# A slot stage in four lanes, second routing in two parts, and nine tiles routed early, in a chain of attention, MoE, slot attention and MoE

## Chip, cores, metric

One core of a Trainium2 chip, one launch, fp32 throughout. The metric is the time of one execution in device microseconds; lower is better.

## The reference

x is 16 batch tiles of 128 tokens by 128 features. Each of four layers takes a layer norm of x and is added back to it.

```python
x = x + block(layernorm(x), cond, ctx)       # adaLN self-attention, cross-attention on 77 rows of ctx (16 heads of 64), gated feed-forward
x = x + moe_a(layernorm(x))                  # shared expert + top 2 of 7, each silu(h g') * (h u') d, inner size 352
x = x + slot_attention(cond, ctx, layernorm(x))
x = x + moe_b(layernorm(x))                  # top 1 of 8, relu(h W1 + b1) W2 + b2, inner size 512

def slot_attention(x_cls, x, noise):         # x = ctx: 77 rows; noise: 128 slots for each batch tile
    k, v = ln(x) @ wk + bk, ln(x) @ wv + bv
    slots = q_mu + exp(q_logsig) * noise
    for _ in range(3):
        prev = slots
        q = ln(slots) @ wq + bq
        attn = softmax(k q' * sqrt(D), over slots) + 1e-8
        attn = attn / attn.sum(over rows)
        slots = (attn' v) @ wu + bu + prev
        slots = gelu(ln(slots) @ w1 + b1) @ w2 + b2 + slots
        slots = ln(slots + x_cls)
    return slots
```

## The kernel before

**Engines and order.** Every engine has its own program, and they meet at semaphores. What each does, and in which order, is written out by hand.

**Attention phase (up to about 550 us).** Iteration i works on four batch tiles at once: self-attention of tile i, cross-attention of tile i-1, the feed-forward and the norm for the router of tile i-2, and the projections of tile i+1. Each iteration has twelve steps k; `FILL` says at which step TensorE puts which product into a rotating bank of PSUM, `AT` at which step the other engines take it. `PLAN` works out, from `FILL`, which use of which bank each is. Iterations 16 and 17 drain the streams. VectorE makes maxima, sums and differences, ScalarE exponentials and copies, GpSimd the normalised probabilities (L1954) and the roots for the norms (L1894). The values of the cross-attention go to DRAM (`v_all`, issued by SyncE at L452) and come back tile by tile (L458). In front of them in SyncE's queue stand `pad_a` and `pad_b`, which fill the row tables `rows_a` and `rows_b` in DRAM.

**Routing.** `routing(x, part)` is a generator on VectorE, one small instruction per step: it takes the best experts of each token, ranks the tokens of an expert (two matmuls on TensorE, `rank_sums`) and gives each row a place in `rows_x`. For MoE a it comes in `PARTS`: tiles 0 to 11 inside the attention phase (`early_routing`, around iteration `RANK_AT` = 14), tiles 12 to 15 behind it. GpSimd scatters the rows to their places (`scatter_one`, L1924), two scatters a tile: those of the early tiles one per step from iteration 16 on, the others before the first blocks. For MoE b all tiles are routed in one part.

**Expert blocks.** `rows_a` has a region of 16 blocks for each expert and is 118 blocks of 128 rows long; 38 of them are computed (`step_a`). `rows_b` is dense: 23 blocks, all computed (`step_b`). SyncE reads where a block starts and whose it is from a table in SBUF and loads rows and weights (`load_blocks`). Behind each block GpSimd keeps its metadata (`meta`), casts the destination to an integer (`dest`), waits for the cast, and scatters the result with an indirect DMA (`send_back`, L2016).

**Slot stage (about 675 to 870 us).** The 16 tiles are four groups of four. `LANES` puts two groups into a lane, and each engine does its steps lane by lane, in a loop over the rounds. For a lane a round is: statistics, root (GpSimd), shift `nbias` (L1707), norm on ScalarE (L1168), turn and logits on TensorE, maxima, exponentials with their sums on ScalarE, shares (L1745 reciprocal, L1748 scale and + 1e-8), update on TensorE, new slots, statistics and norm, the MLP with Gelu (L1194), the sum behind it (L1783), statistics, centring with the gain (L1713) and the slots (L1720). One group of each round is normalised by VectorE (`normed_here`). GpSimd takes the roots with `pow`, keeps slots + bias for the next sum (`keep_slots`, `keep_mid`), and adds MoE a's result to x for half of the tiles; VectorE does the other half (L1832). At the end come x + slots, the norm, the gate (logits taken at L1854), the routing of MoE b, 16 scatters, 23 blocks, and the output.

## Time and profile before

| | |
|---|---|
| median of 3 runs | 981.95 us (979.82 to 982.86) |
| the profiled execution's own time | 977.38 us |
| its span in the trace | 975.6 us |
| mean granted clock of TensorE | 0.889 |
| busy: PE / DVE / ACT / POOL | 770.0 / 584.4 / 509.1 / 388.4 us |
| instructions: PE / DVE / ACT / POOL | 5945 / 1939 / 1078 / 563 |

The span is the time between the first and the last record of the profiled execution; busy times are sums over the instructions of an engine within it. The three runs lie 3.04 us apart from lowest to highest. TensorE is PE, VectorE DVE, ScalarE ACT, GpSimd POOL and SyncE SP.

### The profile page before, as it was taken

To read this page: it belongs to the slowest core of one execution; us is meant where nothing else is said; L and a number is where in the kernel's file an instruction comes from. 1 tells how busy PE (TensorE), PEld (TensorE's weight loads), DVE (VectorE), ACT (ScalarE), POOL (GpSimd) and SP (SyncE) were. 2 spreads that over 40 slices of the span, in tenths; PEclk is the share of its full clock that TensorE was granted. 3 is DMA by queue.
4 is the path that set the end of the run, shared out by engine and by line. 5 is a ranking of instruction groups with operands and counts; after the bars stand their busy time and mean duration, and the time that the engine had idled before them with its cause. 6 is when DMAs were issued, how large, how long until landed. Compare 5 with 4: busy or idle time off the path is not lost.

```text
span 975.6 us, 18523 instructions
## 1 busy us (share of the span) xinstructions
PE 770.0 (79%) x5945; PEld 650.1 (67%) x5945; DVE 584.4 (60%) x1939; ACT 509.1 (52%) x1078; POOL 388.4 (40%) x563
## 2 busy tenths in 40 slices
PE   5898899999999999999777699999363645550692
PEld 5677778788888788887665459998242534340692
DVE  2477778777767666568754443333869687763012
ACT  2566677666677666676444223335364545530461
POOL 1234354333333333332337333656624344225453
PEclk9799999999999999999897799999677677765796
DMA  9592011000011001010001136885300000002463
GB/s 264 182 352 94 1 36 36 14 23 28 2 35 36 15 16 34 2 35 28 14 6 37 68 99 174 253 244 167 106 1 1 0 0 0 0 1 76 127 198 106
DMA packets 43155, 70.95 MB, mean 73 GB/s; under 512 B 5339, under 2 KB 28587, under 8 KB 42651
## 3 DMA queue, kind: packets, MB, share of 16 engines
q1 hardware_dynamic: 39579, 62.64, 21.1%
q0 software_dynamic: 3488, 7.20, 2.1%
q8 instruction: 48, 0.79, 0.3%
q14 instruction: 40, 0.33, 0.1%
HBM read 56.53 MB, written 22.67 MB: 81 GB/s over the span
## 4 chain that ended last, share of the span: by engine, by line
PE 46%; DVE 21%; issue 14%; POOL 9%; ACT 5%; DMA 2%; SPq 2%; DVEq 0%; POOLq 0%; ACTq 0%
PE bank L568 5%; PE bank L839 5%; PE bank L630 5%; PE bank L593 3%; DVE sb_smax L1376 3%; PE bank L583 3%; DVE sb_row_sum L1386 3%; PE bank L618 3%; PE bank L574 2%; PE bank L602 2%; PE bank L847 2%; PE bank L659 2%; PE bank L970 2%; DVE sb_st_all L1680 2%; POOL sb_rstd_all L2052 2%
## 5 line engine op out<-in xcount | busy, mean ns | idle before, releaser
L1954 POOL TENSOR_TENSOR sb_expd<-sb_expd,sb_rden 128x512 f32<-128x512 f32 (+1 forms) x128 | 112.6, 880 | 270.3 <-DVE sb_rden L1390 270.1
L1376 DVE TENSOR_REDUCE sb_smax<-bank 128x4 f32<-128x512 f32 (+1 forms) x128 | 74.1, 579 | 63.6 <-PE bank L593 38.8
L618 PE MATMUL bank<-sb_eye,sb_expd 128*128 128x128 f32 (+1 forms) x512 | 78.2, 280 | 6.9 <-POOL sb_expd L1954 6.2
L1080 ACT ACTIVATE sb_expd<-sb_shifted 128x512 f32<-128x512 f32 (+1 forms) x128 | 69.8, 545 | 21.0 <-DVE sb_shifted L1379 19.6
L1386 DVE TENSOR_REDUCE sb_row_sum<-sb_expd 128x4 f32<-128x512 f32 (+1 forms) x128 | 72.9, 570 | 10.9 <-ACT sb_expd L1080 10.9
L1074 ACT ACTIVATE sb_probT<-bank 128x512 f32<-128x512 f32 (+1 forms) x128 | 74.3, 590 | 9.1 <-PE bank L618 8.8
L618 PEld LDWEIGHTS bank<-sb_eye,sb_expd 128*128 128x128 f32 (+1 forms) x512 | 59.9, 146 | 28.3 <-POOL sb_expd L1954 13.9
L1379 DVE TENSOR_TENSOR sb_shifted<-bank,sb_smax 128x512 f32<-128x512 f32 (+1 forms) x128 | 74.9, 585 | 4.4
L893 PE MATMUL bank<-sb_eye,sb_z_all 128*128 128x128 f32 x96 | 24.3, 420 | 66.9 <-ACT sb_z_all L1168 66.9
L568 PE MATMUL bank<-sb_h1T,sb_watt 128*128 128x128 f32 x512 | 72.6, 289 | 4.5 <-DMA sb_watt<-att_w 2.3
L630 PE MATMUL bank<-sb_probT,sb_v 128*64 128x128 f32 (+1 forms) x1024 | 71.2, 282 | 5.5 <-issue 4.0
L568 PEld LDWEIGHTS bank<-sb_h1T,sb_watt 128*128 128x128 f32 x512 | 64.6, 199 | 9.1 <-DVE sb_xb L1365 3.6
L1168 ACT ACTIVATE sb_z_all<-sb_S,sb_nbias,sb_rstd_all 128x128 f32<-128x128 f32 x84 | 33.6, 481 | 62.0 <-DVE sb_nbias L1707 62.0
L630 PEld LDWEIGHTS bank<-sb_probT,sb_v 128*64 128x64 f32 (+1 forms) x1024 | 55.6, 138 | 14.6 <-issue 5.4
L893 PEld LDWEIGHTS bank<-sb_eye,sb_z_all 128*128 128x128 f32 x96 | 17.5, 214 | 71.5 <-ACT sb_z_all L1168 71.2
L2052 POOL TENSOR_TENSOR sb_rstd_all<-sb_rsq_all,sb_halves 128x8 f32<-128x8 f32 x22 | 36.7, 1669 | 59.2 <-DVE sb_rsq_all L1695 59.1
L839 PE MATMUL bank<-sb_blk_xT,sb_up_w 128*128 128x128 f32 x456 | 57.1, 275 | 0.0
L839 PEld LDWEIGHTS bank<-sb_blk_xT,sb_up_w 128*128 128x128 f32 x456 | 54.0, 192 | 0.0
L2016 POOL DMA_INDIRECT back_a<-sb_blk_y,sb_dest x38 | 37.1, 976 | 40.0 <-DVE sb_blk_y L1657 21.7
L1648 DVE TENSOR_TENSOR sb_hid<-bank,sb_hid 128x384 f32<-128x384 f32 x38 | 21.2, 558 | 51.1 <-ACT sb_hid L1129 32.6
L602 PE MATMUL bank<-sb_g,sb_h2T 128*128 128x308 f32 x128 | 48.4, 461 | 0.0
L1659 DVE TENSOR_TENSOR sb_blk_y<-bank,sb_b2b 128x128 f32<-128x128 f32 x23 | 6.7, 291 | 64.0 <-PE bank L978 52.1
(251 smaller groups left out, 1886.9 us busy)
## 6 DMA issues: line engine op xcount, KB each, us to landing
sb_up_w<-gate_up SPq DMA_DIRECT2D x38, 384.0 KB
rows_a<-pad_a SPq DMA_DIRECT2D x1, 7670.0 KB, 26.8
sb_up_w<-w1b SPq DMA_DIRECT2D x23, 256.0 KB
sb_v<-v_all SPq DMA_DIRECT2D x16, 308.0 KB
v_all<-sb_v_rows SPq DMA_DIRECT2D x9, 512.0 KB, 2.6
sb_blk_x<-rows_a SPq DMA_DIRECT2D x38, 65.0 KB
sb_watt<-att_w SPq DMA_DIRECT2D x4, 512.0 KB, 6.3
sb_picked<-back_a SPq DMA_DIRECT2D x4, 512.0 KB, 5.4
```

The source lines that it names most:

```text
L568: mm = pe.matmul(t[:, c * n:(c + 1) * n], w[:, (4 * half + c) * P:(4 * half + c + 1) * P], src, start=True, stop=True)
L602: pe.matmul(score[u % 2][:, :, 0:C], h2T[:, :], g2[:, QH * j:QH * (j + 1), first:first + C], start=True, stop=True).then_inc(score_done, 1)
L618: mm = pe.transpose(trans[u % 2][0:n, h, :], expd[:, (units_before(i) + u) % EXP_RING, h, 0:n], eye[:, :])
L630: mm = pe.matmul(pvo[DH * r:DH * r + DH, h, :], v[:, 8 * (j // 2) + 2 * h + r, :], probT[0:n, (u - 1 + r) % 2, h, :], start=True, stop=True)
L839: mm = pe.matmul(bank[1 + 2 * j + v][:, c * P:(c + 1) * P], up_w[:, (u + 1) % NSLOT, (j * CA + c) * P:(j * CA + c + 1) * P], blk_xT[:, v, ...
L1074: act.activation(probT[0:n, u % 2, :, :], trans[u % 2][0:n, :, :], ACT.Copy).then_inc(probT_ready, 1)
L1080: act.activation(expd[:, (units_before(i) + u) % EXP_RING, :, 0:n], shifted[:, u % 2, :, 0:n], ACT.Exp, scale=DH ** -0.5).then_inc(exp_don ...
L1376: dve.tensor_reduce(smax[:, u % 2, :], s_in, X, ALU.max).then_inc(max_done, 1)
L1379: dve.tensor_tensor(shifted[:, u % 2, :, 0:n], s_in, smax[:, u % 2, :].unsqueeze(2).broadcast_to([P, QH, n]), ALU.subtract).then_inc(sub_d ...
L1386: dve.tensor_reduce(row_sum[:, u % 2, :], expd[:, (units_before(i) + u) % EXP_RING, :, 0:n], X, ALU.add).then_inc(row_sum_done, 1)
L1954: pool.tensor_tensor(e, e, rden[:, u % 2, :].unsqueeze(2).broadcast_to([P, QH, n]), ALU.mult).then_inc(norm_done, 1)
L2052: pool.tensor_tensor(rstd_all[:, c], rsq_all[:, 0, c], halves[:, c], ALU.pow).then_inc(sl_root, 1)
```

## The change

**Sizes and parts.** MoE a: nine tiles are routed early, seven late. The steps of early routing come one per step k, begin in iteration 10 and end in 13 (`RANK_AT` = 12), and its 18 scatters go out in iterations 14 and 15 from step 4 on (`SCATTER_FROM`). MoE b: two parts, tiles 0 to 11 and 12 to 15; `rows_b` gets a region of 16 blocks for each expert, like `rows_a`, and is 135 blocks long; its table of starts (`start["b"]`) is made as for a, and `w1b` is padded by an expert of zeros. `PLAN` moves the rank matmuls to step 1 of iteration 12 and VectorE's taking of them to step 2; `AT["exp"]` goes from 9 to 5.

**Slot stage.** Four lanes of one group each. `SLOT_STEPS` gives every step a phase; `slot_steps` sorts the steps of all rounds and groups by it, and each engine does its own steps in that order, with the loops written out. Every step waits for its own group: one semaphore for each kind of step. All groups are normalised by ScalarE. The sum behind the MLP is made by TensorE, which multiplies `s_rest` by the identity into the bank of the second layer; statistics and centring read the bank. Shares and the variance + eps are `scalar_tensor_tensor` with a tensor (`least`, `eps`) where a constant was. The sums of x are all VectorE's.

**Routing.** A step of the generator now waits for its result when it is taken up again (`pause`), not before it yields. **Send back.** The destination is cast for each block when its metadata is kept, into a column of its own, and the scatter waits only for the block's result.

```diff
-NREG = EA * REGION + NR - 2 * TOK // P
-
-PARTS = {"a": ((0, 12), (12, B)), "b": ((0, B),)}
+NREG = {"a": EA * REGION + NR - 2 * TOK // P, "b": EB * REGION + NB - TOK // P}
+
+PARTS = {"a": ((0, 9), (9, B)), "b": ((0, 12), (12, B))}
...
-RANK_AT = [last + 2 for _, last in PARTS["a"][:-1]]
+SCATTER_FROM = 4
+RANK_AT = [last + 3 for _, last in PARTS["a"][:-1]]
+SLOT_STEPS = {
+    (-1,): {"add": 7.75},
+    range(0, SLOT_ITERS + 1): {"measure_q": 4.51, "root_q": -0.32, "shift_q": 4.59, "norm_q": 0.96, "turn_q": -6.50,
+        "scale_q": 1.07},
+    range(SLOT_ITERS): {"logits": -6.11, "max": 5.25, "exp": 1.53, "shares": 5.58, "update": -5.64, "updated": 5.96,
+        "keep_mid": 1.75, "measure_m": 6.24, "root_m": 1.42, "shift_m": 6.51, "norm_m": 2.61, "turn_m": -4.62,
+        "scale_m": 3.04, "layer1": -4.37, "gelu": 3.16, "layer2": -3.76},
+    range(-1, SLOT_ITERS): {"measure_o": 7.90, "root_o": 2.80, "centre": 8.12, "slots": 8.38},
+    range(-1, SLOT_ITERS - 1): {"keep_slots": 3.66},
+    (SLOT_ITERS,): {"gate": -5.63, "gated": 8.50, "choose": 9.01, "rank": 69.64, "choice_exp": 70.64, "place": 9.99,
+        "send": 10.95},
+}
+ROUTING_AT = {"choose": (2, 3), "rank": (2, 3), "place": (2, 3), "choice_exp": (3,)}
+
+def slot_steps(*names):
+    found = [(4 * (it + 1) + g + phases[name], name, it, g) for its, phases in SLOT_STEPS.items() for name in names
+             if name in phases for it in its for g in ROUTING_AT.get(name, range(4))]
+    return [step[1:] for step in sorted(found)]
...
-        rows_b = nc.dram_tensor("rows_b", (NB * P, ROW), F32, kind="Internal").ap()
+        rows_b = nc.dram_tensor("rows_b", (NREG["b"] * P, ROW), F32, kind="Internal").ap()
...
+                if step == "layer2":
+                    pe.wait_ge(mid_rest, nth(it, g))
+                    pe.wait_ge(hid_ready, nth(it, g))
+                    for n, b in enumerate(tiles(g)):
+                        pe.matmul(quads(bank[2 * g])[:, n, :], eye[:, :], s_rest[:, b, :], start=True, stop=False)
+                        mm = pe.matmul(quads(bank[2 * g])[:, n, :], hid[:, b, :], w2s, start=False, stop=True)
                     mm.then_inc(mlp_done, 1)
...
-                for part, rank_at in enumerate(RANK_AT):
-                    if (i, k) == (rank_at - 1, N_STEPS - 1) or i == rank_at and k < 6:
-                        steps(early[part], 2)
-                    if i == rank_at and k == AT["rank"]:
-                        steps(early[part], 1)
-                    if i == rank_at + 1:
-                        steps(early[part], 2)
+                for part, rank_at in enumerate(RANK_AT):
+                    if (i, k) == (rank_at - 2, N_STEPS - 1) or i == rank_at - 1:
+                        steps(early[part], 1)
+                    if i == rank_at and k >= AT["rank"] or i == rank_at + 1:
+                        steps(early[part], 1)
...
+                dve.scalar_tensor_tensor(rsq_all[:, 0, c], mv_all[:, c, 1], 1.0, eps[:, c], ALU.mult, ALU.add).then_inc(var_ready[k], 1)
...
+                if step == "shares":
+                    dve.wait_ge(att_exp, nth(it, g))
+                    link(dve.reciprocal(rsum[0:C, c], esum[0:C, c]))
+                    for b in tiles(g):
+                        ins = dve.scalar_tensor_tensor(att[:, b, :], att[:, b, :], rsum[0:C, b:b + 1], least[0:C, :], ALU.mult, ALU.add)
+                    ins.then_inc(att_ready, 1)
...
-                dve.tensor_tensor(group(S, g), quads(bank[2 * g])[:, :, :], group(s_rest, g), ALU.add).then_inc(sum_ready, 1)
...
+                if step == "centre":
+                    scale = es_b[:, :] if it < 0 else R["lnp_g"]
+                    src = x_sb if it < 0 else SUMS
+                    for b in tiles(g):
+                        ins = dve.scalar_tensor_tensor(S[:, b, :], row(src, b), mv_all[:, b, 0:1], scale, ALU.subtract, ALU.mult)
+                    link(ins)
...
-                    if (i, k) == (rank_at + 2, 0):
+                    if (i, k) == (rank_at + 2, SCATTER_FROM):
...
-                    n = N_STEPS * (i - rank_at - 2) + k
-                    if n in range(2 * (last - first)):
+                    n = (N_STEPS - SCATTER_FROM) * (i - rank_at - 2) + k - SCATTER_FROM
+                    if k >= SCATTER_FROM and n in range(2 * (last - first)):
                         scatter_one("a", n % 2, first + n // 2)
...
-                        pool.tensor_copy(meta[:, bass.ds(m, 1), :].rearrange("p a n -> p (a n)"),
-                                         blk_x[:, r, D:ROW]).then_inc(meta_kept[x], 1)
+                        pool.tensor_copy(meta[:, m, :], blk_x[:, r, D:ROW])
+                        stand()
+                        pool.tensor_copy(dest[x][:, m:m + 1], blk_x[:, r, D:D + 1]).then_inc(meta_kept[x], 1)
...
-                        from_one(pool, returned[x][r], 16 * (q - (u == 0)))
-                        stand()
-                        pool.tensor_copy(dest[:, r:r + 1], meta[:, bass.ds(m, 1), 0:1].rearrange("p a n -> p (a n)")).then_inc(
-                            dest_ready[x], 1)
-                        pool.wait_ge(dest_ready[x], m + 1)
                         pool.wait_ge(y_ready[x], m + 1)
...
+                if step == "send":
+                    pool.wait_ge(routed["b"], 1 if g < 3 else 2)
+                    pool.wait_ge(z_normed["q"], nth(it, g))
+                    for b in tiles(g):
+                        scatter_one("b", 0, b)
```

## Rows read from the trace of the kernel before

**Rows 1.** windows, attention: us, then PE PEld DVE ACT POOL busy, PEclk, DMA, GB/s:

```profile
442.00:469.00 27.00, 24.70 (x205) 20.28 (x204) 22.14 (x57) 17.80 (x34) 9.10 (x12) 1.00 0.08 25
469.00:503.50 34.50, 26.17 (x217) 22.39 (x217) 25.82 (x72) 17.12 (x30) 9.98 (x16) 0.85 0.04 11
```

**Rows 2.** timeline of VectorE, attention phase: start, duration, engine, line, operation, wait before it:

```profile
451.92 1.15 DVE L1419 SCALAR_TENSOR_TENSOR sb_rt<-sb_rt,sb_rows 128x84 f32<-128x84 f32 x1
...
524.66 0.34 DVE L1359 TENSOR_SCALAR sb_zC<-sb_x,sb_mv,sb_rstd 128x128 f32<-128x128 f32 x1 [2.71 <-POOL sb_rstd L1894]
...
548.27 0.18 DVE L1415 TENSOR_REDUCE sb_top<-sb_logits 128x4 f32<-128x28 f32 x1 [2.38 <-POOL sb_z_all L1978]
```

**Rows 3.** windows of core 0, one slot round and the scatters behind it:

```profile
758.40:811.50 53.10, 29.92 (x136) 23.32 (x135) 41.71 (x199) 28.07 (x74) 20.04 (x15) 0.69 0.00 0
...
886.40:909.70 23.30, 0.00 (x0) 0.02 (x1) 0.81 (x3) 0.00 (x0) 15.41 (x16) 0.50 0.30 97
```

**Rows 4.** waits of VectorE, 705 to 865 us: total us, count, longest:

```profile
DVE sb_rsum L1745 <- ACT sb_att_or_sent L1183: 10.3, 6, 3.3
```

**Rows 5.** timeline of GpSimd, two scatters of the second expert blocks:

```profile
944.51 0.97 POOL L2016 DMA_INDIRECT back_b<-sb_blk_y,sb_dest  x1 [0.82 <-POOL sb_dest L2011]
...
963.14 0.97 POOL L2016 DMA_INDIRECT back_b<-sb_blk_y,sb_dest  x1 [0.82 <-POOL sb_dest L2011]
```

**Rows 6.** timeline of TensorE, last second-layer matmuls of the second MoE:

```profile
956.55 1.15 PE L978 MATMUL bank<-sb_w2b,sb_hid 128*128 x8 [0.54 <-DVE sb_blk_y L1659]
```

**Rows 7.** timeline of GpSimd, scatters of the first MoE and the first metadata:

```profile
516.46 1.01 POOL L1924 DMA_INDIRECT rows_a<-sb_att_or_sent,sb_slot  x1 [0.16 <-issue]
...
567.01 1.05 POOL L1924 DMA_INDIRECT rows_a<-sb_sent,sb_slot  x1 [18.40 <-DVEq L1506]
...
584.67 0.83 POOL L2004 COPY sb_meta<-sb_blk_x 128x2 f32<-128x2 f32 x4 [7.76 <-DMA sb_blk_x<-rows_a]
```

**Rows 8.** DMA issues: KB each, us from issue to landing:

```profile
rows_a<-pad_a SPq DMA_DIRECT2D x1, 7670.0 KB, 26.8
...
rows_b<-pad_b SPq DMA_DIRECT2D x1, 1495.0 KB, 31.0
```

**Rows 9.** timeline of SyncE: the store of values and the load behind it:

```profile
65.11 0.33 SPq L452 DMA_DIRECT2D v_all<-sb_v_rows  x1
...
80.96 0.78 SPq L458 DMA_DIRECT2D sb_v<-v_all  x2
```

**Rows 10.** timeline of TensorE: first values of tile 0; first block of experts:

```profile
106.33 1.09 PE L630 MATMUL bank<-sb_probT,sb_v 77*64 77x128 f32 x16 [0.53 <-issue]
...
588.37 0.33 PE L819 MATMUL bank<-sb_eye,sb_blk_x 128*128 128x128 f32 x1 [0.78 <-DVE sb_x L1624]
```

**Rows 11.** groups by line, VectorE, 758.4:811.5: busy us, mean ns | idle before:

```profile
L1720 DVE SCALAR_TENSOR_TENSOR sb_S<-sb_S,sb_rstd_all,sb_rows 128x128 f32<-128x128 f32 x16 | 6.4, 475 | 0.5 <-DVE sb_S L1713 0.5
...
L1713 DVE SCALAR_TENSOR_TENSOR sb_S<-sb_S,sb_mv_all,sb_rows 128x128 f32<-128x128 f32 x16 | 4.4, 345 | 0.0
...
L1748 DVE TENSOR_SCALAR sb_att_or_sent<-sb_att_or_sent,sb_rsum 77x128 f32<-77x128 f32 x16 | 3.5, 277 | 0.1
...
L1783 DVE TENSOR_TENSOR sb_S<-bank,sb_s_rest 128x512 f32<-128x512 f32 x4 | 2.7, 689 | 0.2 <-PE bank L929 0.2
```

**Rows 12.** timeline of VectorE, start and end of the slot stage:

```profile
679.13 0.69 DVE L1832 TENSOR_TENSOR sb_x<-sb_x,sb_picked 128x512 f32<-128x512 f32 x1 [7.49 <-DMA sb_picked<-back_a]
...
869.79 0.17 DVE L1707 SCALAR_TENSOR_TENSOR sb_nbias<-sb_mv_all,sb_rstd_all 128x8 f32<-128x8 f32 x1 [1.87 <-POOL sb_rstd_all L2052]
...
877.12 0.29 DVE L1854 TENSOR_TENSOR sb_logits<-bank,sb_rows 128x128 f32<-128x128 f32 x1 [6.13 <-PE bank L953]
```

**Rows 13.** groups by line and form, GpSimd: the roots of four columns:

```profile
L1901 POOL TENSOR_TENSOR sb_rstd_all<-sb_rsq_all,sb_halves 128x4 f32<-128x4 f32 x6 | 6.1, 1021 | 6.2 <-DVE sb_rsq_all L1257 6.2
```

**Rows 14.** timeline of ScalarE, a table load and the Gelu behind it:

```profile
781.28 1.28 ACT L1194 ACT_TABLE_LOAD   x1
782.57 1.27 ACT L1194 ACTIVATE sb_hid<-bank,sb_cols 128x512 f32<-128x512 f32 x2
```

More of the change, by code:

```diff
@@ L722, in rank_sums @@
                 w = N_EXP[x] * (last - first)
[L723 to L725 removed]
+                src = hot[:, N_EXP[x] * first:N_EXP[x] * first + w]
+                pe.matmul(t[:, 0:w], tri[:, :], src, start=True, stop=True)
+                pe.matmul(t[:, w:2 * w], ones[:, :], src, start=True, stop=True).then_inc(
+                    proj_full if x == "a" and part in range(len(RANK_AT)) else rank_done[x], 1)
             def iteration(i, S):
@@ L956, in _ @@
+                if step == "gate":
+                    pe.wait_ge(zT_ready["q"], nth(it, g))
+                    for n, b in enumerate(tiles(g)):
+                        mm = pe.matmul(bank[2 * g + 1][:, n * EB:(n + 1) * EB], zsT[:, b, :], wgate[:, :], start=True, stop=True)
+                    mm.then_inc(lgb_done, 1)
+                if step == "rank":
+                    rank_sums("b", g - 2, bank[2 * (g - 2)])
+            pe.wait_ge(ranks_kept["b"], len(PARTS["b"]))
             pe.wait_ge(ld_moe_b, 32)
@@ L1156, in _, with normed @@
                 from_slot_bank(vu[:, 4 * g:4 * g + 4, 0:D], lambda t: quads(t)[0:C, :, :])
-            def modulated_group(g, done, count, ready, scale, bias):
-                act.wait_ge(done, count)
-                act.activation(group_of(zsT, g), bank[2 * g][:, :], ACT.Identity, scale=scale, bias=bias).then_inc(ready, 1)
-            def normed(lane, stat, count, ready, src=S, dst=zs, groups=2):
-                act.wait_ge(stat, count)
-                for b in tiles(lane)[:4 * groups]:
+            def normed(it, g, k, src, dst):
+                act.wait_ge(shift_ready[k], nth(it, g))
+                for b in tiles(g):
@@ L1753, in updates @@
[L1753 to L1762 removed]
+            links = [0]
```

643 lines of the change are left out of this document (244 added, 399 removed).

## The prediction

> **What bounds the kernel now.** I read the busy time by windows first, then the timelines of single engines where a window is slow, then the groups of instructions and the waits of the slot stage, last the DMA issues. No engine bounds the whole kernel. The attention phase runs on TensorE, one batch tile per iteration of about 26 us, except where VectorE falls behind: iteration 15 takes 34.5 us with 72 VectorE instructions, against 27.0 us for the one before it [rows 1]. The extra instructions are the early routing of twelve tiles, two per step; several of them take over 1 us where a neighbour of the same size takes 0.3, since both of their inputs are in SBUF and GpSimd is reading too [rows 2]. In the two drain iterations 16 and 17 GpSimd has 24 scatters in its queue, and two things wait behind them: zC for 2.71 us, and the end of the phase for 2.38 us [rows 2].
>
> The slot stage is bound by VectorE plus its waits. One round of 53.1 us has 41.7 us of VectorE, 28 of ScalarE, 20 of GpSimd, and TensorE at a mean clock of 0.69 between its two levels [rows 3]. The waits come from two lanes of eight tiles that leave VectorE nothing to do while a lane's exponentials run [rows 4]. Then comes a serial tail: last norm, gate, routing, 16 scatters with TensorE at a standstill for 23.3 us [rows 3]. In the expert blocks of the second MoE GpSimd is last: its scatters are 2.07 us apart (9 steps between the two rows), and the last one starts 5.4 us after TensorE has finished [rows 5, 6].
>
> **Attention phase.** (a) With nine tiles, routing takes its steps one at a time in iterations 11 to 13, and iteration 15 has none: 34.5 falls to the 27.0 of its neighbour, which carried 12 routing instructions and shows that this many are hidden: -7.5 (bounds -9.5, 0). (b) Iterations 11 to 13 get some 12 each on a VectorE that has 27 - 22 = 5 us left: +0.5 each, +1.5 (0, +4). (c) 18 scatters now start in iteration 14 at step 4, one per step, eight in 14 and eight in 15. A scatter takes 1.01 us and starts 0.16 us behind GpSimd work [rows 7]; what hides it is GpSimd's idle time, about 18 of 27 us; behind it queue the normalisation of the probabilities and the roots of the norms. +1 per iteration, +2 (0, +8). (d) Iterations 16 and 17 lose 22 of 24 scatters: the two waits above end, down to the usual root latency: -1.8 and -2.2, together -4 (-5, -2). (e) rows_b is laid out in regions, so its pad grows from 1495 KB (23 blocks) to 8775 KB (135 blocks). The first pad moves at 7670 / 26.8 = 286 KB/us, so both, 9165 KB, hold the queue for 32 us [rows 8]; the store of values issued at 65.11 us behind them lands only at 80.96, when SP issues the load that waited for it [rows 9]. 7280 KB more are 25 us more: that store lands near 106, its load near 109, and TensorE wants these values at 106.3 us [rows 10]. Nothing else is ready in its queue then: +3 (0, +6). Sum: -7.5 + 1.5 + 2 - 4 + 3 = -5.
>
> **Start of the first blocks.** The late part of routing has seven tiles, 14 scatters for 8. They start at 567.01 and the eighth has ended at 576.9 (584.67 less 7.76 of idle), 1.28 us for each; six more end 7.7 us later, at 584.6 [rows 7]. From there to GpSimd's first metadata it is 7.8 us today, so the blocks would be there at 592.4, and TensorE comes at 588.37 [rows 7, 10]: +4 at most. But part of the 7.8 us is four weight loads (1536 KB, 5 us at the rate above) that by then are done: +2 (0, +4). Inside the blocks TensorE is the bound and nothing changes; at the end the destination is cast earlier, -0.5.
>
> **Slot stage.** VectorE is busy 41.7 us in a round [rows 3]. Off it go the sums after the MLP, 2.7 (TensorE adds s_rest by the identity) and the normalisation of one group, 4 x 0.27 = 1.1 (ScalarE's now) [rows 11]. On it come the tensor form of shares, 4.4 for 3.5 by the row of the nearest instruction of that form [rows 11]; some 14 small instructions of about 0.1, since blocks of four columns replace blocks of eight, 1.5; the waits for its own results in each group, about 1.1, 4.4 in all; and 0.9 for shares that meet GpSimd, half of what the slots instruction pays for that (6.4 against 4.4) [rows 11]. Statistics and centring read PSUM instead of SBUF; the trace has no statistics from PSUM, and I take them as equal (0, +1 a round). Sum 45.6 us a round, 11.4 a group. At the start each group has, at the same rates, two residual sums 1.8, statistics 1.5, centring 1.3, slots 1.3, statistics 1.5: 7.4 us; at the end one sum and a shift: 1. Together 4 x (7.4 + 3 x 11.4 + 1) = 171 us of VectorE. From its first sum at 679.1 to the last shift at 869.9 [rows 12] it is 190.7 us today. What is left as wait in the new order: about 3 us while the first group fills, 5 in the last round, where only one group's chain runs. In the middle the longest gap is from the query shift to the maxima (four norms, turn, scale, four matmuls). For two groups the like chain (norm, turn, copy, gate) took 7.3 us [rows 12]; for one I take 5.5, and between the two steps stand measure_o, updated, centre and measure_m, 5.8 us. So it just closes. 171 + 8 = 179, -11.7 us (-18, +4).
>
> What could break this: a root on GpSimd takes 1.02 us for four columns [rows 13], hidden by the 1.3 us of shares. ScalarE alternates Gelu and Exp in every group, eight table loads a round against two: that makes its round 28.1 + 6 x 1.28 + 1.7 (the fourth group's normalisation) = 37.5 us, 9.4 a group, under 11.4 [rows 3, 14]. The row shows the next activation 0.01 us after a load [rows 14]. The Trainium skill, "ScalarE: Activation LUTs", section What ACT_TABLE_LOAD costs, gives 1.28 us for the load and some 1.38 us of drain with it; this trace has the first number and not the second.
>
> **Tail.** Today the first scatter comes 16.5 us after the last shift and the sixteenth 19 us later. Part 0 (12 tiles) is placed only behind "gated" of group 3: 5.7 for gate, 0.3, ranks on TensorE 0.9, 13 placing instructions 3.3, GpSimd 0.8: first scatter at +11. Part 1 is ready by +15, while part 0's twelve still run. So all 16 scatters stay exposed and only their start moves: -5.6 (-9, -2). The larger table is made beside them.
>
> **Second blocks.** The wait for its own cast goes, and the wait for `returned`. The cast costs 0.82 us of idle time before each scatter, against 0.16 behind work without such a wait [rows 5, 7]. Cycle 0.97 + 0.3 + 0.2 = 1.5, below TensorE's. TensorE ends at 957.7 [rows 6]; with 0.3 for the result, 0.8 and 0.97 the last scatter ends at 959.8, not 964.1: -4.3, and TensorE's own waits of 0.5 go: -4.8 (-6, 0 if the 0.82 stays).
>
> **Sum.** -5 + 2 - 0.5 - 11.7 - 5.6 - 4.8 = -25.6 us. It is made on the profiled execution (977.4 us, span 975.6), which lies 4.6 below the median of the runs; I carry the difference to the median: 981.95 - 25.6 = **956 us**.
>
> **Rivals.**
> 1. The waits are halved only. Today 53.1 - 41.7 = 11.4 us of a round are not VectorE work [rows 3]. If TensorE sits at its lower level and an in-order queue hands the delay on, about 13 more us remain over three rounds: 969. For it: clock 0.69, two to three times more handovers; against it: shorter gaps for TensorE. Chance 0.20.
> 2. No change: all 11.4 us a round stay and VectorE has 45.6 of its own, 57 a round: +34 - 8 = +26, 982. Chance 0.05.
> 3. Slower: VectorE and GpSimd block each other. The slots instruction, with two SBUF inputs, costs 0.40 beside GpSimd's keep_slots, the like centring 0.27 [rows 11]. Shares and eps get two SBUF inputs as well, five such places in a group. If each waits for one whole GpSimd instruction (1.0 to 1.3 us, less what is in the sum), that is 3.6 us per group, x 12 = 43: 999. It decides from 2.1 us per group. The Trainium skill, "SBUF — State Buffer", section Who interferes with whom, has that rule (an exclusive lock for the whole instruction); the rows agree in kind. Chance 0.04.
> 4. ScalarE becomes the bound: with 1.4 us of idle behind each load it needs 9.4 + 2 x 1.4 = 12.2 us a group, 0.9 over VectorE, x 12: 967. The page on ScalarE above would have it so. Chance 0.05.
> 5. Better: the pads and the scatters in 14 and 15 cost nothing (-5), the clock rises and the middle has no wait (-7): 944. Chance 0.11.
>
> **How the numbers follow.** The sum as worked out has 0.55 and a range of its own of 948 to 964. Eight times in ten: 943 to 973, which leaves out rivals 2 and 3 and the ends of 1 and 5. 0.3%, about 3 us, is what a measurement can tell: faster 0.91, within it 0.05 (rival 2), slower 0.04 (rival 3).
>
> **What would show it.** Iteration 15 at 27 us; the store of values landing near 106 and TensorE waiting before that pv matmul; the first block transpose 2 us later against the end of the phase; one max per group every 11.4 to 12 us; in the wait list of VectorE few waits for ScalarE; shares at about 0.27 each; first b scatter 11 us behind the last shift; GpSimd's gap before a back_b scatter gone, and scatters at TensorE's pace. It is wrong if groups follow each other at over 13 us, if slots and shares show long durations beside GpSimd, or if iterations 14 and 15 grow.

## The result, and the profile after

The changed kernel takes 970.08 us (median of 4 runs, 969.70 to 974.45); the kernel before takes 982.40 in the same comparison. The ratio is 0.9879 (95% interval 0.9854 to 0.9903): 12 us faster, where 26 were forecast. The sign is right and the time lies inside the range, but about half of the gain is missing. The profiled execution took 969.92 us, with a span of 968.0.

The spans differ by 7.6 us. The kernel before had been profiled in one of its shorter executions (977.4 against a median of 982.4), so stages are compared by the two traces, and the whole by the medians. Each column of the table is one execution, and the same stage of one kernel differs between executions; where that matters, the spread is given.

The table cuts the span at instructions that both traces have, and gives what each stretch became. The last two columns are of runs told of below: the changed kernel again in another set of runs (r1), and, in that set, the changed kernel with one step of GpSimd moved (r2).

| stretch, us | before | predicted | changed | r1 | r2 |
|---|---|---|---|---|---|
| start to first instruction of late routing | 548.3 | -5.0 | -7.5 | -6.9 | -8.7 |
| to last scatter of the first MoE's blocks | 124.8 | +1.5 | +10.2 | +0.3 | +1.7 |
| to the first sum of x | 6.0 | 0 | +0.3 | +0.4 | +0.3 |
| slot stage, to the last shift | 190.7 | -11.7 | -0.8 | -0.2 | -11.8 |
| to the first scatter of the second MoE | 16.6 | -5.6 | -6.2 | -6.2 | -6.2 |
| to the last scatter of its blocks | 76.7 | -4.8 | -4.1 | -3.4 | -3.3 |
| to the end | 12.5 | 0 | +0.5 | +0.4 | +0.5 |
| span | 975.6 | -25.6 | -7.6 | -15.6 | -27.6 |

Two stretches hold the whole miss: the first MoE's blocks start late, and the slot stage gained nothing.

**Slot stage.** One round of the changed kernel, between two maxima of one group, by windows (columns as in rows 1):

```profile
746.66:798.37 51.71, 34.99 (x169) 27.86 (x167) 44.54 (x205) 37.78 (x85) 22.44 (x21) 0.74 0.00 1
```

Against 53.10 us [rows 3] that is 1.4 less, with VectorE busier (44.54 us for 41.71). The groups of instructions by line of the same window, VectorE (busy us, mean ns):

```profile
L1705 DVE SCALAR_TENSOR_TENSOR sb_att_or_sent<-sb_att_or_sent,sb_rsum,sb_least 77x128 f32<-77x128 f32 x16 | 5.6, 407 | 0.1
...
L1736 DVE SCALAR_TENSOR_TENSOR sb_S<-sb_S,sb_rstd_all,sb_rows 128x128 f32<-128x128 f32 x16 | 4.6, 347 | 0.0
...
L1674 DVE SCALAR_TENSOR_TENSOR sb_nbias<-sb_mv_all,sb_rstd_all 128x4 f32<-128x4 f32 x8 | 4.6, 571 | 0.1
```

The eight shifts of four columns (L1674) take 571 ns on average, where one of eight columns takes 0.17 us [rows 12]. The mean mixes two kinds: three of the eight take 1.25 or 1.26 us, the other five 0.16. The timelines of one group, VectorE, GpSimd, ScalarE and TensorE in turn:

```profile
764.34 0.16 DVE L1674 SCALAR_TENSOR_TENSOR sb_nbias<-sb_mv_all,sb_rstd_all 128x4 f32<-128x4 f32 x1
...
764.62 1.14 DVE L1705 SCALAR_TENSOR_TENSOR sb_att_or_sent<-sb_att_or_sent,sb_rsum,sb_least 77x128 f32<-77x128 f32 x4
765.67 1.25 DVE L1674 SCALAR_TENSOR_TENSOR sb_nbias<-sb_mv_all,sb_rstd_all 128x4 f32<-128x4 f32 x1
...
773.23 0.69 DVE L1698 TENSOR_REDUCE sb_lgmax<-bank 77x4 f32<-77x512 f32 x1 [0.67 <-PE bank L926]
```

```profile
764.45 1.02 POOL L1936 TENSOR_TENSOR sb_rstd_all<-sb_rsq_all,sb_halves 128x4 f32<-128x4 f32 x1 [0.47 <-DVE sb_rsq_all L1668]
765.43 1.47 POOL L1951 TENSOR_TENSOR sb_s_rest<-sb_S,sb_cb 128x512 f32<-128x512 f32 x1
```

```profile
766.96 1.65 ACT L1162 ACTIVATE sb_z_all<-sb_S,sb_nbias,sb_rstd_all 128x128 f32<-128x128 f32 x4 [0.79 <-DVE sb_nbias L1674]
```

```profile
771.28 1.92 PE L926 MATMUL bank<-sb_zsT,sb_kq 128*77 128x128 f32 x8
```

GpSimd's keep_mid (L1951) begins at 765.43 and ends at 766.90. VectorE's query shift, both inputs in SBUF, begins at 765.67 and ends at 766.92, with it. Behind it wait the norm of the queries, the turn, the logits and the maxima. So it is in eleven of twelve groups (1.25 us ten times, 1.11 once); in the twelfth keep_mid comes a little earlier against them, and the shares are held instead, 2.15 us for the four. VectorE and GpSimd:

```profile
750.91 2.15 DVE L1705 SCALAR_TENSOR_TENSOR sb_att_or_sent<-sb_att_or_sent,sb_rsum,sb_least 77x128 f32<-77x128 f32 x4
```

```profile
751.66 1.26 POOL L1951 TENSOR_TENSOR sb_s_rest<-sb_S,sb_cb 128x512 f32<-128x512 f32 x1
```

**First blocks.** VectorE's and ScalarE's timelines at the end of the shared expert, and TensorE's behind it:

```profile
581.10 0.69 DVE L1604 TENSOR_TENSOR sb_x<-sb_x,bank 128x512 f32<-128x512 f32 x1 [9.66 <-remote]
```

```profile
581.15 1.08 ACT L1112 ACTIVATE sb_hid<-bank 128x512 f32<-128x512 f32 x2 [10.51 <-remote]
```

```profile
572.52 3.60 PE L824 MATMUL bank<-sb_zsT,sb_moe_w 128*128 128x512 f32 x8
583.12 5.49 PE L812 MATMUL bank<-sb_moe_w,sb_s_rest 128*128 128x128 f32 x24 [7.01 <-DVE sb_s_rest L1611]
589.39 0.47 PE L843 MATMUL bank<-sb_eye,sb_blk_x 128*128 128x128 f32 x1 [0.78 <-DVE sb_x L1604]
```

Both engines wait for TensorE's matmuls, which by their records are over at 572.7 and 576.1. The semaphore counts that they wait for come at 581.07 to 581.19, three within 0.12 us ("remote": the profile ties the release to no instruction). Meanwhile GpSimd issues its fourteen scatters, from 560.80 to 577.63, and SyncE, which waits until all of them have landed, starts to load rows at 580.10:

```profile
580.10 10.27 SPq L511 DMA_DIRECT2D sb_blk_x<-rows_a  x5
```

TensorE has nothing to do, its granted clock falls, and the next 24 matmuls take 5.5 us. The windows show the clock, the third last number, at 0.50, its lower level of 1.2 GHz:

```profile
576.00:584.00 8.00, 0.99 (x5) 0.88 (x5) 1.97 (x3) 1.08 (x2) 3.23 (x11) 0.69 0.24 66
584.00:590.00 6.00, 5.09 (x23) 4.50 (x22) 0.72 (x2) 0.10 (x1) 0.00 (x1) 0.50 0.00 0
```

The kernel before has one such wait, of 2.3 us, with eight scatters.

**Attention.** Iterations 14 and 15 of the changed kernel by windows:

```profile
439.85:469.67 29.82, 29.25 (x253) 24.43 (x253) 19.56 (x53) 20.59 (x38) 15.01 (x20) 1.00 0.11 34
469.67:500.41 30.74, 22.88 (x213) 19.40 (x213) 19.72 (x54) 16.73 (x30) 17.98 (x24) 1.00 0.09 29
```

**Tail and second blocks.** VectorE's last shift, GpSimd's first scatter of routing b and its last of the blocks:

```profile
871.98 0.16 DVE L1674 SCALAR_TENSOR_TENSOR sb_nbias<-sb_mv_all,sb_rstd_all 128x4 f32<-128x4 f32 x1 [1.24 <-POOL sb_rstd_all L1936]
```

```profile
882.39 1.05 POOL L1814 DMA_INDIRECT rows_b<-sb_sent,sb_slot  x1 [10.56 <-DVEq L1489]
...
955.03 0.95 POOL L1902 DMA_INDIRECT back_b<-sb_blk_y,sb_dest_b  x1 [0.74 <-issue]
```

### The profile page after: what moved, and what is told of

Same layout as the page of the kernel before. It is cut to its first block, busy times and chain, and to the rows that moved or that the text cites. A ratio compares the mean times of both kernels' runs of the same rounds, so it can differ in the third digit from the quotient of the medians.

```text
span 968.0 us, 18773 instructions
## 1 busy us (share of the span) xinstructions
PE 795.7 (82%) x6045; PEld 672.2 (69%) x6045; DVE 592.9 (61%) x1989; ACT 536.7 (55%) x1109; POOL 392.2 (41%) x583
## 4 chain that ended last, share of the span: by engine, by line
PE 48%; DVE 23%; issue 10%; DMA 7%; ACT 5%; POOL 4%; SPq 3%; another core or an unknown queue 1%; DVEq 0%; POOLq 0%; ACTq 0%
PE bank L591 5%; PE bank L653 4%; DMA v_all<-sb_v_rows 4%; PE bank L863 4%; PE bank L616 4%; PE bank L606 3%; PE bank L597 3%; DVE sb_smax L1352 2%; PE bank L641 2%; DVE sb_st_all L1661 2%; PE bank L625 2%; PE bank L969 2%; PE bank L682 2%; PE bank L977 2%; DVE sb_row_sum L1362 2%
## 5 line engine op out<-in xcount | busy, mean ns | idle before, releaser
L1936 POOL TENSOR_TENSOR sb_rstd_all<-sb_rsq_all,sb_halves 128x4 f32<-128x4 f32 x44 | 44.7, 1016 | 92.9 <-DVE sb_rsq_all L1668 92.9
L1362 DVE TENSOR_REDUCE sb_row_sum<-sb_expd 128x4 f32<-128x512 f32 (+1 forms) x128 | 72.9, 570 | 11.3 <-ACT sb_expd L1079 11.2
L931 PE MATMUL bank<-sb_vu,sb_att_or_sent 77*128 77x129 f32 x96 | 21.7, 395 | 48.9 <-DVE sb_att_or_sent L1705 48.9
L863 PE MATMUL bank<-sb_blk_xT,sb_up_w 128*128 128x128 f32 x456 | 59.7, 283 | 0.0
L1162 ACT ACTIVATE sb_z_all<-sb_S,sb_nbias,sb_rstd_all 128x128 f32<-128x128 f32 x96 | 39.5, 482 | 31.7 <-DVE sb_nbias L1674 31.7
L863 PEld LDWEIGHTS bank<-sb_blk_xT,sb_up_w 128*128 128x128 f32 x456 | 56.5, 199 | 0.0
L1902 POOL DMA_INDIRECT back_a<-sb_blk_y,sb_dest_a x38 | 37.0, 973 | 45.1 <-issue 23.7
L931 PEld LDWEIGHTS bank<-sb_vu,sb_att_or_sent 77*128 77x128 f32 x96 | 18.4, 285 | 51.5 <-DVE sb_att_or_sent L1705 51.5
L616 PE MATMUL bank<-sb_k1T,sb_q1T 64*128 64x128 f32 x512 | 38.4, 289 | 5.6 <-DVE sb_shifted L1355 5.0
```

Source lines behind the costliest of these rows:

```text
L616: mm = pe.matmul(score[(u + r) % 2][:, h, :], q1T[p, 4 * (j // 2) + h, :], k1T[p, 4 * (j // 2) + h, :], start=True, stop=True)
L863: mm = pe.matmul(bank[1 + 2 * j + v][:, c * P:(c + 1) * P], up_w[:, (u + 1) % NSLOT, (j * CA + c) * P:(j * CA + c + 1) * P], blk_xT[:, v, ...
L1362: dve.tensor_reduce(row_sum[:, u % 2, :], expd[:, (units_before(i) + u) % EXP_RING, :, 0:n], X, ALU.add).then_inc(row_sum_done, 1)
```

## Experiments

Medians and ratios are those of a set of runs made on one chip, against the kernel before in the same set; each of the four sets was on another chip. Experiments 1 to 4 are one set, 5 to 7 a second, the first three of 8 a third, and its last four a fourth.

**1. The changed kernel again, without an edit.**

> The changed kernel once more, beside which the others of this set are read. Question: is the wait at the end of the shared expert a fixed cost? In its first trace the counts of TensorE that ScalarE and VectorE wait for come at 581.1 us, 8.4 us behind the matmuls by their records, while the four weight loads of the blocks and 14 scatters are under way, and TensorE's granted clock falls to 0.5 behind it. Theory C (collision of that moment's transfers): the wait comes again, 6 to 10 us, since everything is issued at the same moments; 970 us. Rival (a chance stall of one execution): it is gone or of quite another size, and the trace's last block ends some 9 us earlier.

970.33 us, ratio 0.9879 (0.9845 to 0.9913). The wait came again, 9.54 us on VectorE, and the first block was turned at 592.3. So it is no chance of one execution.

**2. keep_mid in front of root_m.** GpSimd takes it while VectorE reads PSUM.

```diff
-        "keep_mid": 1.75, "measure_m": 6.24, "root_m": 1.42,
+        "keep_mid": 1.41, "measure_m": 6.24, "root_m": 1.42,
```

> GpSimd's keep_mid (1.27 us, two inputs in SBUF) moves from behind root_q to in front of root_m, where VectorE reads PSUM. Theory H (holding): in the changed kernel the query shift of a group takes 1.25 us instead of 0.16, ends with keep_mid each time, and the norm of the queries stands behind it. Then the shift falls to 0.16, the chain to the maxima begins 1.1 us earlier, and groups follow each other every 11.7 to 12.0 us instead of 12.8: 9 to 12 us in all, 958 to 961. Rival Q (TensorE's order and clock set the pace): the shift is short, but VectorE waits as much longer for the logits: within 2 us of the changed kernel.

958.99 us, ratio 0.9780 (0.9745 to 0.9816), 11.3 us under the changed kernel of that set. Its query shifts, by groups of instructions on VectorE, and one round by windows:

```profile
L1674 DVE SCALAR_TENSOR_TENSOR sb_nbias<-sb_mv_all,sb_rstd_all 128x4 f32<-128x4 f32 x8 | 1.3, 157 | 0.0
```

```profile
769.50:814.62 45.12, 30.31 (x168) 23.37 (x166) 40.19 (x205) 36.94 (x84) 21.40 (x20) 0.85 0.01 1
```

And keep_mid beside the centring, GpSimd and then VectorE, of its repetition (8 below):

```profile
769.80 1.27 POOL L1951 TENSOR_TENSOR sb_s_rest<-sb_S,sb_cb 128x512 f32<-128x512 f32 x1 [0.30 <-DVE sb_S L1714]
```

```profile
769.64 1.12 DVE L1730 SCALAR_TENSOR_TENSOR sb_S<-bank,sb_mv_all,sb_rows 128x128 f32<-128x128 f32 x4
```

The centring, with one input in PSUM, keeps its 1.12 us beside it. One phase number was worth about as much as the whole change (11.3 us beside 12). The holding theory stands; the rival, that TensorE's order sets the pace, falls.

**3. Twelve tiles early, with the schedule of before.**

```diff
-PARTS = {"a": ((0, 9), (9, B)), ...
-SCATTER_FROM = 4
-RANK_AT = [last + 3 ...
+PARTS = {"a": ((0, 12), (12, B)), ...
+SCATTER_FROM = 0
+RANK_AT = [last + 2 ...
```

with the positions of rank and exp in FILL and AT, and the two steps at a time of early routing, as before.

> Twelve tiles routed early, two steps at a time, scatters in iterations 16 and 17, as in the kernel before; all else as changed. By the traces the attention phase gets its 7.5 us back, and 8 scatters instead of 14 stand before the blocks. Theory C (the stall at the end of the shared expert comes from having more scatters and the weight loads at the same moment): the stall falls back to the 2.1 us of before, so that the blocks begin about as early as in the changed kernel and the sum is +0 to +2 us against it. Rival (the stall is of the code, not of the transfers): it stays at 8 us, +7 us against the changed kernel.

971.48 us, ratio 0.9881 (0.9840 to 0.9922): 1.2 more than the changed kernel of its set. The first late routing comes at 550.1 instead of 544.1, and the longest late count is 0.9 us. Where the counts are late, nine tiles give back at the start of the blocks what they won in the attention phase.

**4. Weights of the first blocks behind the scatters.** SyncE issues the four weight loads last.

```diff
-                for m in range(NSLOT):
-                    load_weights(x, m, places[m][1])
                 sp.wait_ge(scattered[x], 16 * scatters)
                 for m in range(NSLOT):
                     load(x, src, m, places[m][0])
+                for m in range(NSLOT):
+                    load_weights(x, m, places[m][1])
```

(for the first MoE alone).

> In front of the first blocks of the first MoE, SyncE waits for the scatters and loads the rows first, and issues the four weight loads (1536 KB) behind them. Theory C: with the weight loads away from the end of the shared expert the stall of 8.4 us is gone and TensorE's clock stays up (another 5 us), but weights land some 6 us after the last scatter, at 586: the blocks begin near 586 instead of 589.4 at full clock, -5 to -8 us in all. Rival (scatters alone or the fetch of code make the stall): it stays, and the blocks begin later by the load's 5 us, +3 to +5.

971.26 us, ratio 0.9895 (0.9863 to 0.9927). VectorE waits 9.46 us as before, and the block comes at 590.7. The weight loads are not the cause: theory C falls.

**5. Shares and eps with constants.**

```diff
-  dve.scalar_tensor_tensor(att[:, b, :], att[:, b, :], rsum[0:C, b:b + 1], least[0:C, :], ALU.mult, ALU.add)
+  dve.tensor_scalar(att[:, b, :], att[:, b, :], rsum[0:C, b:b + 1], 1e-8, ALU.mult, ALU.add)
```

and the variance + eps likewise.

> The changed kernel with shares and variance + eps written with constants again (tensor_scalar) instead of the tensors least and eps. By the rows shares go from 0.35 to 0.28 us each, 0.28 us a group, 3.4 us of VectorE in all. If VectorE's work sets the pace of the groups it is 3 us faster than the changed kernel (967); if the chain from the query shift to the maxima does (it ends in a wait of 0.67 us for TensorE), nothing moves by more than 1 us. Rival: the constant forms hold GpSimd's roots and the kernel is slower by 3 us or more, which would be the reason for the tensor forms.

970.41 us, ratio 0.9881 (0.9852 to 0.9909): no difference in the median. Its shifts and shares on VectorE:

```profile
L1674 DVE SCALAR_TENSOR_TENSOR sb_nbias<-sb_mv_all,sb_rstd_all 128x4 f32<-128x4 f32 x8 | 4.9, 612 | 0.7 <-POOL sb_rstd_all L1936 0.6
...
L1705 DVE TENSOR_SCALAR sb_att_or_sent<-sb_att_or_sent,sb_rsum 77x128 f32<-77x128 f32 x16 | 3.5, 278 | 0.1
```

Shares take 3.5 us a round where undisturbed tensor forms take 4.5 (the kernel of 2), and all twelve shifts are held, but for 1.03 to 1.10 us instead of 1.25: keep_mid, which in the changed kernel begins 0.3 us before the shares are done and takes 1.47 us, here takes 1.27. Groups follow every 12.6 instead of 12.8 us, and the slot stage of this trace takes 186.3 us, against 189.5 to 191.2 in the seven traces that have the tensor forms and keep_mid in its old place: about the 3.4 us expected. The median does not show them. Five executions lie 5.2 us apart, and the set has no run of the unedited changed kernel, so whether the constant forms gain 3 us in all stays open; the rival, that they cost 3 us, falls.

**6. Scatters in two batches, and scatters held back.** In the first GpSimd waits behind the seventh late scatter until seven have landed; in the second it waits for the end of the shared expert ahead of all fourteen.

```diff
+                    if (b, k) == (first + 3, 0):
+                        pool.wait_ge(scattered["a"], 16 * (2 * b + 1))
```

```diff
+            pool.wait_ge(sh_added, G)
             for b in range(first, last):
```

> The changed kernel, with GpSimd waiting once, behind the seventh of the fourteen late scatters, until all have landed (some 3 us). Theory S (the scatters in flight hold TensorE's counts once they are many): the stall of 8.4 us shrinks to the size seen with eight scatters, 2 us or less, TensorE's clock stays up, and the blocks begin when the scatters have landed, near 583 instead of 589: -5 to -9 us. Rival (the stall belongs to this place of the program whatever the scatters do): it stays, and the whole is 0 to 3 us slower.

> The changed kernel, with all fourteen late scatters held back until the shared expert is done. If scatters cause the stall, no count of TensorE is late in this stretch (none above 1 us), the shared expert ends near 577, and the scatters run alone behind it for 18 us: blocks begin near 598, +7 to +9 us against the changed kernel. If they don't cause it, the stall stays, the shared expert ends at 588 and the blocks begin at 609: +18 to +20.

Two batches: 969.94 us, ratio 0.9864 (0.9834 to 0.9894), none of the 5 to 9 us expected in the median. The long wait is gone from its place, and one of 5.4 us stands at the last down product. It ends when the second batch has landed, at which SyncE loads the rows (VectorE, then SyncE):

```profile
588.74 0.69 DVE L1604 TENSOR_TENSOR sb_x<-sb_x,bank 128x512 f32<-128x512 f32 x1 [5.39 <-remote]
```

```profile
588.74 3.03 SPq L511 DMA_DIRECT2D sb_blk_x<-rows_a  x5
```

The first block is turned at 590.8. Counted from the first instruction of late routing that is 44.0 us, against 48.6 and 48.2 in the two traces of the unedited kernel, and the stretch to the last scatter of the blocks takes 129.2 us against 135.0 and 134.5: the 5 us are there in this trace, but its attention phase took 546.9 us against 540.8 and 544.1. What the batches are worth is therefore not settled by the median.

Held back: 986.78 us, ratio 1.0047 (1.0026 to 1.0068). VectorE's timeline, and TensorE's at the first block:

```profile
573.86 0.69 DVE L1604 TENSOR_TENSOR sb_x<-sb_x,bank 128x512 f32<-128x512 f32 x1 [1.29 <-PE bank L812]
```

```profile
603.97 0.45 PE L843 MATMUL bank<-sb_eye,sb_blk_x 128*128 128x128 f32 x1 [22.36 <-DMA sb_blk_x<-rows_a]
```

No count is late without scatters in flight, at the price of scatters that nothing hides. The 16 us above the changed kernel (of the other sets) are more than the 7 to 9 expected: the shared expert is done only at 582.3, not near 577, so that the scatters run from 583.15 and the first block comes at 604 instead of 598; TensorE stands still for 22 us before it.

Could this run simply have had no late counts, whatever the scatters did, as the runs of 8 below? One sign says no. In the second MoE scatters are in flight too when SyncE reads the table of starts, and its first weight load comes 4.5 to 4.7 us behind the table in every trace of the changed kernel and its variants from the result and experiments 1 to 6, and 3.0 to 3.2 us in all those of 8. In this run it is 4.68 (VectorE, then SyncE):

```profile
906.45 0.17 DVE L1509 TENSOR_TENSOR sb_start_b<-sb_bex,sb_rows 1x23 int32<-1x23 f32 x1
```

```profile
911.13 3.29 SPq L519 DMA_DIRECT2D sb_up_w<-w1b  x4
```

So the scatters are needed for the late counts. That they are not sufficient is what 8 shows.

**7. The edit of send_back alone, in the kernel before** (the diff is that of the change).

> The kernel before with the edit of send_back alone: a column of destinations for each block, cast with the metadata, no wait for the cast or for the returned rows. As in the prediction: scatters of the second blocks at TensorE's pace, the last one 4 to 5 us earlier, the first MoE's blocks unchanged but 0.5 at their end: 4.8 us faster than before (977.5). Rival (the wait is only renamed, since the indirect DMA waits for the block's result anyway): within 1 us of before.

977.90 us, ratio 0.9952 (0.9932 to 0.9973), 3.8 us faster. Most scatters start 0.58 to 0.72 us behind the metadata instead of 0.82 behind their own cast, and they follow each other every 1.9 us. From the first scatter of the second MoE to the last of its blocks it is 72.4 us instead of 76.7. The term holds.

**8. Ten tiles; logits first; pad in parts** (each with keep_mid moved as in 2).

```diff
-PARTS = {"a": ((0, 9), (9, B)), ...
+PARTS = {"a": ((0, 10), (10, B)), ...
```

```diff
-    range(SLOT_ITERS): {"logits": -6.11, ...
+    range(SLOT_ITERS): {"logits": -6.38, ...
```

```diff
+                if 2 <= i < 7:
+                    part = slice((i - 2) * NREG["b"] * ROW // 5, (i - 1) * NREG["b"] * ROW // 5)
+                    sp.dma_start(*(v.rearrange("(p n) d -> p (n d)", p=P)[:, part] for v in (rows_b, A["pad_b"]))).then_inc(zeroed, 16)
...
```

> keep_mid as in e1_keep_mid_early, and ten tiles routed early instead of nine: routing moves one iteration back, its 20 scatters go out in iterations 15, 16 and 17, and 12 instead of 14 stand before the blocks. Theory S (TensorE's counts are late while back-to-back scatters are in flight, from the seventh or eighth on until all have landed): the scatters end 2.5 us earlier, the stall is 2.5 us or more shorter, and the attention phase is up to 2 us longer: -1 to -4 us against e1_keep_mid_early (ratio to before 0.976, 0.972 to 0.977). Rival: the drain iterations lose as much by the scatters in them: ratio 0.978 or above.

> keep_mid as in e1_keep_mid_early, and TensorE makes the logits of a group in front of the first MLP layer instead of behind it. In e1_keep_mid_early VectorE still waits for the logits, 1.0 us in some groups, none in others. Theory Q (the chain from the query shift to the maxima still sets part of the pace): those waits end, -3 to -5 us against e1_keep_mid_early (ratio to before 0.973 to 0.975). Rival (VectorE's own work is the bound now, and ScalarE's Gelu, later by the logits' 1 us, moves the wait to the second layer's statistics): within 1.5 us, 0.977 to 0.980.

> keep_mid as in e1_keep_mid_early, and the 8775 KB of pad_b issued in five parts behind the value transfers of iterations 2 to 6 instead of in one behind pad_a. In the traces with the whole pad the stretch from the first use of the values to the next iteration takes 0 to 4 us more than before (30.5 to 34.5 us), 1.6 in the mean. Theory E (the pad delays the store of values past the moment TensorE wants them): the stretch is 30.5 us again, values of later iterations still come in time, -1 to -2 us in the median against e1_keep_mid_early (ratio to before 0.976 to 0.977). Rival (the parts delay the later values instead): 0 to +5 us.

Ten tiles 954.13, ratio 0.9743 (0.9700 to 0.9785); logits first 950.12, ratio 0.9713 (0.9676 to 0.9750); pad in parts 949.55, ratio 0.9694 (0.9664 to 0.9723). By their ratios the last came 7 us better than expected and logits first 2. The traces show that no count is late in any of the three, though logits first has the same instructions up to the end of the first MoE as kernels that had the wait, pad in parts differs there only in the transfers of the pad, and both issue the same scatters at the same moments (logits first from 560.18 to 577.00). So theory S falls as stated: scatters are not enough. Ten tiles came inside the range expected, but not for the reason given, since there was no late count to shorten. The changed kernel and that of 2 were run once more beside two combinations.

> The changed kernel for the third time. Theory P (the stall goes with the chip or the placement of a call, not with the program): if e11 and e12 of this call show no stall, this one shows none, its blocks begin near 583 and it takes 961 to 964 us against a before of about 979; if they show it, this one does, and takes 970. Rival (program): it shows the 8.4 us and 970 us whatever e11 and e12 show.

> e1_keep_mid_early for the second time, for comparison inside one call. Whatever the stall does, it is 10 to 12 us faster than the changed kernel of this call (theory H). Under theory P its blocks begin when those of r1_changed_third do.

> keep_mid in front of root_m, logits in front of the first MLP layer, and pad_b in five parts; nine tiles. If the parts add up: 0 to -3 us for the logits and -1 to -2 us for the pad against r2_keep_mid_again. Rival: both are within what a call differs from another, and it is within 1 us of r2_keep_mid_again.

> As e11_all_nine, with ten tiles routed early. In e8_ten the drain iterations were some 5 us longer than with nine tiles and two scatters fewer stood before the blocks. If this call has the stall, ten tiles are 1 to 4 us faster than nine; if it has none, 2 to 4 us slower.

The unedited changed kernel took 962.51 us here, ratio 0.9823 (0.9799 to 0.9848), as theory P had it, and its trace has no late count. VectorE's and TensorE's rows at the place of the wait, and the windows:

```profile
573.10 0.69 DVE L1604 TENSOR_TENSOR sb_x<-sb_x,bank 128x512 f32<-128x512 f32 x1 [1.29 <-PE bank L812]
```

```profile
582.55 0.30 PE L843 MATMUL bank<-sb_eye,sb_blk_x 128*128 128x128 f32 x1 [1.71 <-DMA sb_blk_x<-rows_a]
```

```profile
584.00:590.00 6.00, 5.87 (x52) 5.65 (x51) 1.88 (x5) 2.17 (x6) 1.60 (x5) 1.00 0.56 160
```

keep_mid moved: 950.07, ratio 0.9693 (0.9671 to 0.9715), again 12.4 us under the changed kernel of its set. All parts with nine tiles: 950.58, ratio 0.9704 (0.9679 to 0.9730); with ten: 954.14, ratio 0.9715 (0.9679 to 0.9751). Logits first and pad parts together add nothing that can be told, and ten tiles are no better where the counts are in time. The version to keep is the changed kernel with keep_mid moved.

## Why the prediction was off

**Slot stage, forecast -11.7, came -0.8.** The step that failed is the term for VectorE instructions that meet GpSimd, "0.9 for shares that meet GpSimd": I looked for the cost of two SBUF inputs only in large instructions, priced what a held instruction loses itself, and put the small ones at nothing. The one that was held is the smallest there is, the query shift, 1.09 us in ten of the groups (0.95 in another), and it stands at the head of the chain to the maxima. Eleven groups of it make 12 us, the whole gain of the stage. With keep_mid moved the same stage takes 179.2 and 178.8 us for the 179 forecast (kernel of 2 and r2), but that it agrees so well is in part luck. A round was to take 45.6 us each time; between the second and third maxima of a group it takes 45.1 to 46.8, between the first and second 46.8 to 51.7. VectorE is busy for 151.6 us of the stage in both, where the 171 worked out, less the 13 in them for waits for its own results, make 158: the work was put too high by about what the waits were put too low. The mechanism was my rival 3, whose size of 3.6 us a group was three times too large and whose chance of 0.04 was too small, and which named shares and eps and not the shift; below its turning point of 2.1 it does not reverse the sign, and that middle case I had left out. The Trainium skill, "SBUF — State Buffer", section Who interferes with whom, has this rule, that a VectorE instruction with two SBUF inputs contends with a GpSimd instruction that reads SBUF, and that one with at most one SBUF input, outside the two-port modes, does not. The shift (held) and the centring from PSUM (1.12 us beside keep_mid) agree with the two halves. GpSimd's root does not fit the first: it has two SBUF inputs and takes 1.02 us, yet the shares beside it, with two SBUF inputs, take 1.14 us for four (764.62 above), as the slots instruction does with GpSimd idle. Here the measurement decides:

```profile
761.49 1.14 DVE L1736 SCALAR_TENSOR_TENSOR sb_S<-sb_S,sb_rstd_all,sb_rows 128x128 f32<-128x128 f32 x4
```

**Start of the first blocks, forecast +2, came +8.5, and with the low clock behind it +10.2.** The scatters themselves were priced rightly: the first rows are there at 582, and in the runs without late counts the stretch costs +0.3 (r1) and +1.7 (r2). What I had no term for is that TensorE's counts come late while they are in flight. The sum has it at nothing; it measured 8.4 us of lateness, and the first block came 8.5 us later where 2 were forecast. The row was there in the trace of before (ScalarE, 2.3 us, "remote"), and I read past it:

```profile
578.34 0.60 ACT L1113 ACTIVATE sb_hid<-bank 128x512 f32<-128x512 f32 x1 [2.26 <-remote]
```

It is a matter of the set of runs as well as of the program: the changed kernel took 970.1 and 970.3 in two sets with it and 962.5 in one without. That it needs scatters in flight is shown (6); why it is there in some sets and not in others is open, since sets differ in chip and time at once. The two misses add up to more than the whole: with neither of them r2 takes 950.07 us, 6 below the forecast of 956.

**Attention, forecast -5, came -7.5.** The -7.5 is one execution: in the ten traces with nine tiles and the whole pad the phase is 1.4 to 8.7 us shorter than in the trace of before, 6.2 in the mean, so the sum of -5 was about right. Its parts were read less well. (a) The window of 27.0 us that I took for an iteration was a part of iteration 14. By the starts of the same norm in both traces an undisturbed iteration takes 29.3 to 29.6 us, and 14 and 15 took 32.2 and 34.5; they now take 29.8 and 30.7: -6.1 for the -7.5. Iteration 15 goes with TensorE's granted clock, which I had left out: the row of before has 0.85 [rows 1], the changed kernel 1.00. Of the ten traces just named two have 1.00 (29.6 and 30.7 us) and eight 0.84 to 0.95 (31.7 to 33.4). (b) +1.5, as forecast. (c) The scatters in 14 and 15 are hidden but for what is in these numbers. (d) -4.4 for -4. (e) +3 was forecast for the pad. Its store landed as worked out: SyncE issues the load behind it at 105.59. The price varies between executions; TensorE's waits from 90 to 125 us in the changed kernel (us, times, longest):

```profile
PE bank L653 <- DMA sb_v<-v_all: 2.4, 1, 2.4
```

In other runs it is between nothing (5) and 3.9 (two batches in 6). The stretch between the first two norms into `sb_zC` takes 30.8 us in the kernel before and 0 to 4 us more in the eight traces of the changed pad up to experiment 6, 1.6 in the mean. In the trace above it takes only 0.2 more; where the wait is 3.2 us or more, the granted clock of the stretch falls to 0.93 to 0.97 as well.

**Tail, forecast -5.6, came -6.2; second blocks, -4.8, came -4.1.** The first scatter comes 10.4 us behind the last shift for the 11 worked out. Each was read from the right rows. The wait for the cast went, and scatters now follow TensorE. Three roundings in the working are off without weight: 4 x 42.6 is 170.4 and not 171, eight scatters up to 576.9 take 1.24 us each and not 1.28, and half of 6.4 less 4.4 is 1.0 and not 0.9.

**Rivals.** Rival 4 did not come: ScalarE is busy 37.8 us a round for the 37.5 worked out, and behind a table load the next activation starts 0.01 us later (ScalarE's timeline):

```profile
757.75 1.28 ACT L1190 ACT_TABLE_LOAD   x1
759.04 0.69 ACT L1190 ACTIVATE sb_hid<-bank,sb_cols 128x512 f32<-128x512 f32 x1
```

Rival 1 named the right size for the wrong reason: a round has 7.2 us that are not VectorE work instead of 11.4, of which 3.7 are waits for TensorE; with the hold gone these are 1.4 (r2), at a clock of 0.85 instead of 0.74. Rival 5 did not come: the clock was 0.74 in the round and the scatters and pad cost what is said above. The forecast sum of -25.6 is near what the program does where neither the hold nor the late counts are (r2: -27.6 by the spans, -30.3 by the medians).

## What to carry to other kernels

Before moving steps of two engines against each other, list for each place which operands of VectorE are in SBUF and what GpSimd runs beside it, small instructions first: price a hold by what is queued behind the held instruction, not by its own length. Where a schedule is a table of phases, try every place of the long GpSimd steps; one number was worth 11 to 12 us here. And read each unexplained wait of the trace before, however short: the change may multiply it.

## What the hardware showed that I had not expected

A VectorE instruction with two SBUF inputs on 128x4 elements, 0.16 us alone, takes 1.25 us when a GpSimd addition with two SBUF inputs (128x512, 1.27 to 1.47 us) is under way, and ends with it; beside GpSimd's root on 128x4 (1.02 us) VectorE's shares lose nothing (1.14 us for the four). So how long a GpSimd instruction takes does not say how long it holds VectorE.

TensorE's semaphore counts can come up to 8.4 us behind its matmuls while scatters issued every 1.26 us are in flight. They then come together, within 0.12 us, and in the six traces of nine tiles that have them 0 to 1.0 us after SyncE, which waits for all scatters, starts to load the rows. With the same program the lateness was there in the sets of runs that gave 970 us and absent in the one that gave 962.5. In the latter SyncE issues the first weight load of the first MoE 3.4 us behind the table, in the former 5.1 to 5.3; with the scatters held back it was 3.4 in one of the former sets too, so this delay as well goes with scatters in flight.
